# Two-layer modulated transformer on one core: the last batch's query and key rows move to another buffer, and every engine gets a new written-out order

## The chip, the cores and the metric

The kernel runs on one core of one Trainium2 chip. The metric is the device time of one execution in microseconds (us). TensorE is PE in the profile, its weight loads PEld, VectorE DVE, ScalarE ACT, GpSimd POOL, SyncE SP.

## What is computed

Input x has 8 batches of 512 rows of 128 floats, all in float32. Two layers follow one another, and in both every sublayer is of the same form: `x = x + gate * sublayer(layernorm(x) * (1 + scale) + shift)`, where shift, scale and gate are rows of `silu(c) @ wmod`, one set for each batch.

- Layer 0, attention: 16 heads of 8 elements, queries and keys rotated, softmax over 512 keys.
- Layer 0, experts: 8 experts with `silu(h @ w0) * (h @ w1) @ wo`, weighted by a softmax over the best two of 8 gate logits.
- Layer 1, gated unit: `qk = silu(normed @ W_qk + b_qk)`, `q = qk * gamma0 + beta0`, `k = qk * gamma1 + beta1`, `sim = q.T @ k / 512` (a 256x256 matrix per batch), `attn = softmax(sim)`; with `v, gate = silu(normed @ W_hidden + b_hidden)` the result is `(v * sum(attn, -1)) * gate @ W_out + b_out`.
- Layer 1, feed-forward: each batch is one expert's share: `gelu(h @ w1[b] + b1[b]) @ w2[b] + b2[b]`.

## The kernel before, in words

The program works batch by batch, in four stages: P (normalise, project, rotate, and split queries and keys into three bf16 parts), A (attention), B (experts), C (all of layer 1). A step such as C6.sim is step `sim` of stage C for batch 6; a number behind it is a group, chunk or half (C6.dn0 is the first half of the down-projection, C7.up2 the third chunk of the up-projection). Stages of several batches run beside one another: while PE is in the experts of batch b it also works on the attention of batch b+1 and on layer 1 of an earlier batch.

Nothing decides at run time what comes next. `SLOTS` (line 69) holds for each step and engine a list of positions, batch after batch (and within a batch, instance after instance, as `INSTANCES` lists them); `order_of` (line 305) sorts them, and `walk` (line 543) emits the steps of an engine in that order. Only the order of the numbers counts. Steps that exist in one batch alone (for instance `C.out0` and `C.upb`, in the last batch) have numbers for the others that emit nothing. Waits between engines are on semaphores, written by `after(engine, name, batch, count)`; an engine that waits holds up all that stands behind it in its order.

PSUM has eight banks: `sm` and `se` (two banks each, the two score products of attention), `pv` (weighted values), `wp` (experts), `m0` (shared by A and B, `shared_ab`) and `m1` (shared by P and C, `shared_pc`). In the last batch attention is over, so stage C of batch 7 uses other banks than `m1`: `qk` goes to `wp` and `pv`, the four hidden chunks to `sm` and `se`, `sim` to `m0`, `out` to `wp`, `up` to `sm` and `se`, `dn` to `m0`, `m1`, `wp`, `pv`.

Steps that the change and the prediction touch, in the tail:

- `q_and_k` (line 632): from the silu'd rows z, four instructions per half (lines 644, 645, 647, 649) write q and k to the tile `kq` of 128 x 2 x 4 x 256. It is on DVE for batch 7, on POOL for the others.
- `gl`, the gelu output of the feed-forward, is the same memory as `kq` (line 464). So `q_and_k` of batch b waits for both halves of the down-projection of batch b-1, which reads `gl` (line 635).
- `eo` (line 410), 128 x 8 x 2 x 128, holds the output weights of the experts. It is loaded once and read by step B.down (lines 1030 to 1031), last in batch 7.
- `sim` (line 1078) multiplies q by k on PE (L1088), `simmax`, `simexp` and `simsum` (lines 1748, 1341, 1755) make its softmax and the scaled output weights `wos`, `hids` (line 1726) makes v times gate (`vg`, L1730 and L1735), `c_out` (line 1102) multiplies them, `res` (line 1773) adds the residual.
- `dn` (line 1141) is the down-projection (L1159, in the last batch L1149), `fin` (line 1799) its last addition, on DVE; the output store `outp` and then the load of the next down-projection's weights `loadd` stand behind it on SP; `w2g` (line 1933) scales those weights on POOL.
- `out0` (line 1092) and `upb` (line 1117) start the sums of batch 7 in PSUM ahead of time: x2 through the identity, and the bias rows of `up`.
- `stats3`, `rstd3`, `xn3`, `xT3`, `nT3` are the second normalisation: statistics on DVE, power on POOL (L1854), scaling on DVE in batch 7 (L1584), transposes on PE (L889), modulation on ACT (L1234); then `up` (L1134 in batch 7), `upa` and `upg` (L1782, L1792).

Steps of the start: `P.xT` (L889), `P.v` (L915), `P.xn` on ACT for batches after the first (L1249), `e0hi` and `e1hi` (L1196, L1201) round the expert weights on ACT, `e1lo` (L1847) takes the rest on POOL; `A.max` (L932 on PE, L1557 on DVE) is the pass that finds each row's largest score, `A.exp` (L956 on PE, L1269 on ACT) the pass that exponentiates.

The last part of the order of PE, read off `SLOTS`, before:

```
C6.up0 B7.down71 C6.up1 C6.up2 C6.up3 C7.xT C7.qk0 C6.dn0 C7.qk1 C6.dn1 C7.hid0 C7.out0 C7.hid2
C7.upb0 C7.hid1 C7.hid3 C7.sim C7.upb1 C7.out C7.xT3 C7.up0 C7.up1 C7.up2 C7.up3 C7.dn0 C7.dn1
```

## Time and profile before

| | |
|---|---|
| median of 3 runs | 1085.66 us (1082.01 to 1087.82) |
| the profiled execution | 1092.12 us |
| its span, first to last instruction | 1089.9 us, mean granted TensorE clock 0.930 |
| busy: PE, PEld, DVE, ACT, POOL | 85%, 47%, 71%, 60%, 39% |

The profiled execution is 6.46 us (0.6%) above the median of the three; 2.2 us of its time lie outside the span. The profile's views used below are the page (busy shares, and the span in 40 slices), stretches (busy time and granted clock of each engine in a window), the chain of waits that ended last, the timeline (instructions in order, with the idle time of the engine ahead of them and what ended it) and the list of who waited for whom. A granted clock of 1.00 is 2.4 GHz and 0.50 is 1.2 GHz.

### The profile page before, as it was taken

Reading aid. Unit: us, or ns where it says so; the run is one execution under the profiler, and the core shown is the slowest. Engines: PE = TensorE matmul, PEld = TensorE weight load, DVE = VectorE, ACT = ScalarE, POOL = GpSimd, SP = SyncE. Lnnn points to the kernel's source line nnn. Section 1 sums busy time; section 2 is a strip of 40 time slices with the busy share of each in tenths; the row PEclk is TensorE's granted clock in tenths of the full one; section 3 lists DMA queues with packets and bytes.
Section 4 is the critical chain, followed back from the end, with each engine's and each line's share of the span. In section 5 each row is a group of like instructions: output and inputs, shape, how many; then the busy total and the mean of one; then the engine's idle time right before and its main releaser. Section 6 shows DMA issues by size and latency. Waiting matters only on the chain. (4 is left out here: it accounts for less than half of the span.)

```text
span 1089.9 us, 15616 instructions
## 1 busy us (share of the span) xinstructions
PE 926.0 (85%) x5176; PEld 513.5 (47%) x5176; DVE 776.2 (71%) x1467; ACT 655.6 (60%) x1176; POOL 426.8 (39%) x537
## 2 busy tenths in 40 slices
PE   4247678997899799998999998999998999889785
PEld 2111135443444355554554654446464466368553
DVE  6566678677756877788867777888878765546665
ACT  1236664666656758668768576866856756745441
POOL 2161042226112815574134364653556244454300
PEclk9558988999999989999999999999999899979876
DMA  8520304001300140111300014150001000010010
GB/s 233 154 66 30 60 30 98 33 1 55 59 2 1 32 101 9 34 43 58 62 1 13 16 61 86 59 105 11 1 25 33 2 21 16 20 35 1 18 34 10
DMA packets 54536, 47.09 MB, mean 43 GB/s; under 512 B 12393, under 2 KB 50025, under 8 KB 53114
## 3 DMA queue, kind: packets, MB, share of 16 engines
q1 hardware_dynamic: 53898, 45.85, 16.7%
q8 instruction: 42, 0.69, 0.3%
q14 instruction: 36, 0.29, 0.1%
q10 hardware_dynamic: 560, 0.26, 0.1%
HBM read 30.97 MB, written 14.73 MB: 42 GB/s over the span
## 5 line engine op out<-in xcount | busy, mean ns | idle before, releaser
L1557 DVE TENSOR_REDUCE negmax<-scores_for_max 128x2 f32<-128x1024 f32 x252 | 307.9, 1222 | 73.7 <-PE scores_for_max L932 71.3
L1269 ACT ACTIVATE probs<-scores 128x1024 f32<-128x1024 f32 x256 | 262.0, 1023 | 91.8 <-PE scores L956 90.7
L1030 PE MATMUL shared_ab<-eo,mu 128*128 128x128 f32 x1024 | 143.4, 283 | 9.0 <-ACT scaled L1383 4.8
L1030 PEld LDWEIGHTS shared_ab<-eo,mu 128*128 128x128 f32 x1024 | 129.0, 193 | 45.2 <-issue 28.1
L966 PE MATMUL weighted_values<-probs,vaug 128*32 128x512 f32 x1024 | 142.3, 630 | 1.0 <-ACT probs L1269 0.9
L1953 POOL TENSOR_TENSOR acc<-acc,scaled 128x512 f32<-128x512 f32 x55 | 71.2, 1294 | 178.8 <-ACT scaled L1383 178.7
L1692 DVE SCALAR_TENSOR_TENSOR mu<-th,expert_units 128x512 f32<-128x512 f32 x112 | 76.7, 685 | 72.4 <-ACT th L1311 71.6
L932 PE MATMUL scores_for_max<-ks,qs 48*128 48x512 bf16 x504 | 102.6, 404 | 27.8 <-DVE negmax L1557 19.4
L572 PE MATMUL expert_units<-hb_hi,e_lo 128*128 128x512 f32 x224 | 112.2, 501 | 15.3 <-DVE mu L1692 9.7
L956 PE MATMUL scores<-qs,ks 51*128 51x512 bf16 x512 | 102.2, 396 | 20.8 <-ACT probs L1269 17.7
L1311 ACT ACTIVATE th<-expert_units 128x512 f32<-128x512 f32 x112 | 66.8, 597 | 78.8 <-PE expert_units L574 77.2
L1698 DVE TENSOR_TENSOR mu<-mu,expert_units 128x512 f32<-128x512 f32 x112 | 76.5, 683 | 31.1 <-PE expert_units L574 30.5
L1383 ACT ACTIVATE scaled<-shared_ab,pick 128x128 f32<-128x128 f32 x220 | 68.5, 365 | 44.8 <-PE shared_ab L1030 41.4
L573 PE MATMUL expert_units<-hb_lo,e_hi 128*128 128x512 f32 x224 | 89.9, 402 | 0.0
L574 PE MATMUL expert_units<-hb_hi,e_hi 128*128 128x512 f32 x224 | 89.6, 400 | 0.0
L572 PEld LDWEIGHTS expert_units<-hb_hi,e_lo 128*128 128x128 f32 x224 | 42.6, 190 | 87.2 <-DVE mu L1698 28.6
L932 PEld LDWEIGHTS scores_for_max<-ks,qs 48*128 48x128 bf16 x504 | 24.6, 94 | 111.8 <-DVE negmax L1557 70.9
L956 PEld LDWEIGHTS scores<-qs,ks 51*128 51x128 bf16 x512 | 25.0, 94 | 88.2 <-ACT probs L1269 47.6
L1909 POOL CAST mpart<-negmax 128x16 bf16<-128x16 f32 x32 | 8.8, 274 | 142.0 <-DVE negmax L1557 141.9
L574 PEld LDWEIGHTS expert_units<-hb_hi,e_hi 128*128 128x128 f32 x224 | 42.9, 192 | 10.1
L573 PEld LDWEIGHTS expert_units<-hb_lo,e_hi 128*128 128x128 f32 x224 | 43.3, 193 | 0.9 <-issue 0.5
L1139 PE MATMUL shared_pc<-xdn,w 128*128 128x512 f32 x56 | 32.1, 657 | 9.4 <-ACT u L1366 8.9
(320 smaller groups left out, 1590.8 us busy)
## 6 DMA issues: line engine op xcount, KB each, us to landing
parts_d<-parts SPq DMA_DIRECT2D x15, 384.0 KB, 2.5
qs<-parts_d SPq DMA_DIRECT2D x14, 384.0 KB, 6.1
ks<-parts_d SPq DMA_DIRECT2D x14, 384.0 KB, 9.8
w<-in_L_ffn_w SPq DMA_DIRECT2D x16, 256.0 KB, 3.9
parts_d<-parts SPq DMA_DIRECT2D x15, 256.0 KB, 2.7
...
```

Of the source, the lines that this page charges most:

```text
L572: nc.tensor.matmul(out_ap, w_lo, x_hi, start=True, stop=False)
L573: nc.tensor.matmul(out_ap, w_hi, x_lo, start=False, stop=False)
L574: return nc.tensor.matmul(out_ap, w_hi, x_hi, start=False, stop=True)
L932: last = nc.tensor.matmul(max_bank(b, g, n)[:, 512 * m:512 * (m + 1)], qs[at, b % 2, p, t * P:(t + 1) * P], ks[at, b % 2, p, :], start=Tru ...
L956: last = nc.tensor.matmul(se[:, 512 * m:512 * (m + 1)], ks[at, b % 2, p, kt * P:(kt + 1) * P], qs[at, b % 2, p, :], start=True, stop=True)
L966: last = nc.tensor.matmul(pv[32 * j:32 * j + 32, :], vaug[:, kt, PAIRS * (j // 2) + GP * g + j % 2, :], probs[:, kt % 2, j % 2, j // 2, :] ...
L1030: last = nc.tensor.matmul(m0[:, at], mu[:, (2 * e + f) % 4, at], eo[:, e, f, :], start=(f == 0), stop=(f == HALVES - 1))
L1269: nc.scalar.activation(probs[:, kt % 2, j, :, :].rearrange("p m s -> p (m s)"), se[:, :], ACT.Exp)\
L1557: V.tensor_reduce(negmax[:, g % 2, :, n], max_bank(b, g, n)[:, :].rearrange("p (m s) -> p m s", m=2), AX, ALU.max, negate=True)\
L1692: V.scalar_tensor_tensor(out=mu[:, u % 4, :], in0=th[:, u % 2, :], scalar=1.0, in1=w0p(b, u), op0=ALU.add, op1=ALU.mult).then_inc(sig["b_u ...
L1698: V.tensor_tensor(mu[:, u % 4, :], mu[:, u % 4, :], w1p(b, u), ALU.mult).then_inc(sig["b_mu"], 1)
L1953: G.tensor_tensor(acc[:, :, :], acc[:, :, :], scaled[:, :, :], ALU.add).then_inc(sig["b_acc"], 1)
```

## The change

Two edits of the code, and a new set of positions.

1. In batch 7, q and k are written to the memory of `eo`, and `sim` reads them there. The first half of `q_and_k` waits for the last read of `eo` (16 counts of `b_down`) and no longer for the down-projection of batch 6. Since batch 7's `gl` still lies in `kq`'s memory, the wait for batch 6's down-projection moves to the first `upg` of batch 7.
2. The second set of modulation columns on PE waits until DVE has copied the first.
3. All of `SLOTS` is new. The set of steps on each engine is the same; of 1288 steps on PE 831 stand at another place, by at most 9 places; on DVE 412 of 834, by up to 47; on ACT 506 of 824, by up to 19; on POOL 150 of 250, by up to 10; on SP 75 of 114, by up to 9.

```diff
@@ SLOTS, some of the lines @@
-    ("P", "stats"): dict(dve=(78, 184, 192, 215, 297, 363, 549, 571)),
+    ("P", "stats"): dict(dve=(76, 142, 205, 226, 295, 361, 549, 571)),
-    ("P", "xT"): dict(pe=(27, 54, 68, 181, 325, 532, 658, 881)),
+    ("P", "xT"): dict(pe=(30, 60, 72, 178, 324, 531, 662, 880)),
-    ("P", "e0hi"): dict(act=(25, 32, 33, 34, 39, 40, 41, 59)),
+    ("P", "e0hi"): dict(act=(20, 21, 24, 27, 38, 45, 46, 50)),
-    ("C", "stats2"): dict(dve=(361, 481, 555, 701, 780, 853, 936, 1000)),
+    ("C", "stats2"): dict(dve=(363, 482, 555, 703, 781, 853, 934, 1000)),
-    ("C", "qk"): dict(pe=(471, 477, 595, 605, 821, 829, 944, 965, 1070, 1074, 1176, 1183, 1262, 1269, 1325, 1327)),
+    ("C", "qk"): dict(pe=(472, 480, 594, 603, 822, 828, 945, 961, 1069, 1073, 1177, 1183, 1262, 1274, 1325, 1326)),
-    ("C", "sim"): dict(pe=(526, 637, 874, 1002, 1111, 1215, 1301, 1335)),
+    ("C", "sim"): dict(pe=(526, 637, 873, 1002, 1111, 1215, 1299, 1332)),
-    ("C", "dn"): dict(pe=(598, 600, 813, 818, 952, 958, 1065, 1067, 1172, 1174, 1257, 1259, 1326, 1328, 1343, 1344)),
-    ("C", "fin"): dict(dve=(517, 519, 646, 649, 735, 738, 808, 811, 882, 884, 937, 939, 1006, 1012, 1031, 1032)),
+    ("C", "dn"): dict(pe=(597, 599, 812, 819, 952, 958, 1065, 1067, 1172, 1175, 1258, 1259, 1327, 1333, 1343, 1344)),
+    ("C", "fin"): dict(dve=(515, 519, 645, 650, 735, 738, 809, 811, 883, 885, 938, 939, 1012, 1016, 1031, 1032)),
-    ("C", "rstd3"): dict(pool=(107, 134, 172, 198, 223, 237, 261, 272)),
-    ("C", "w2g"): dict(pool=(23, 146, 168, 196, 217, 239, 254, 271)),
+    ("C", "rstd3"): dict(pool=(104, 138, 171, 197, 222, 238, 263, 271)),
+    ("C", "w2g"): dict(pool=(34, 136, 167, 201, 220, 234, 257, 272)),
-    ("C", "upb"): dict(pe=(8, 9, 13, 14, 15, 16, 17, 18, 31, 34, 37, 43, 49, 51, 1332, 1336)),
-    ("C", "out0"): dict(pe=(6, 7, 10, 11, 12, 33, 50, 1330)),
+    ("C", "upb"): dict(pe=(1, 3, 4, 5, 6, 7, 13, 14, 15, 16, 17, 18, 19, 20, 1336, 1337)),
+    ("C", "out0"): dict(pe=(2, 8, 9, 10, 11, 12, 41, 1334)),
...
@@ code @@
+        def kq_of(b):
+
+            return eo[:, :, :, :].rearrange("p e f d -> p (e f d)").rearrange("p (a t n) -> p a t n", a=2, t=NT) if b == LAST else kq
+
         def q_and_k(eng, E, b, p):
             after(eng, "c_qs", b, p + 1)
             if p == 0:
-                after(eng, "c_dn", b - 1, 2)
+                if b == LAST:
+                    after(eng, "b_down", b, 2 * NEX)
+                else:
+                    after(eng, "c_dn", b - 1, 2)
                 if b == 0:
                     eng.wait_ge(s_small, 3)
-            at = slice(2 * p, 2 * p + 2)
+            at, kq = slice(2 * p, 2 * p + 2), kq_of(b)
...
                     pe.wait_ge(s_silu, 2 * (L + 1))
                     if L:
                         pe.wait_ge(s_cr, 16 * N_CONST)
+                        pe.wait_ge(s_cols, 2)
...
-                        last = nc.tensor.matmul(dst[:, n * QK:(n + 1) * QK], kq[:, 0, t, n * P:(n + 1) * P],
-                                                kq[:, 1, t, :], start=(t == 0), stop=(t == NT - 1))
+                        last = nc.tensor.matmul(dst[:, n * QK:(n + 1) * QK], kq_of(b)[:, 0, t, n * P:(n + 1) * P],
+                                                kq_of(b)[:, 1, t, :], start=(t == 0), stop=(t == NT - 1))
...
             def upg(b, c):
                 after(dve, "c_ut", b, c + 1)
                 if b == LAST:
+                    if c == 0:
+                        after(dve, "c_dn", b - 1, 2)
```

The last part of the order, after, for PE and DVE (`fin` is C6.fin0 and C6.fin1; on POOL `C7.w2g` goes from ahead of `C7.rstd3` to behind it):

```
PE   C6.up3 C7.xT C7.qk0 C7.qk1 C6.dn0 C7.hid0 C7.hid2 C7.hid1 C7.hid3 C7.sim C6.dn1 C7.out0 C7.out
     C7.upb0 C7.upb1 C7.xT3 C7.up0 C7.up1 C7.up2 C7.up3 C7.dn0 C7.dn1
DVE  C6.upg3 C7.qks0 C7.qkgb0 C7.qks1 C7.qkgb1 C7.hids0 C7.hids2 C6.fin0 C7.hids1 C7.simmax C7.hids3
     C6.fin1 C7.simsum C7.keep C7.res C7.stats3 C7.xn3 C7.keep3 ...
```

On DVE before it was `C6.upg3 C6.fin0 C7.qks0 C7.qks1 C7.qkgb0 C7.qkgb1 C7.hids0 C6.fin1 C7.hids2 C7.hids1 C7.simmax C7.hids3 C7.simsum`, the rest as after. At the start, PE's `P1.v A0.max00 P1.proj1 A0.max01 ... A0.max07 P2.xT A0.max10` takes the place of `A0.max00 P1.v A0.max01 P1.proj1 A0.max02 A0.max03 A0.max04 P2.xT A0.max05 ... A0.max10`. When batch 7 enters stage B, DVE's `C5.upa3 C6.stats2 C5.upg3 B7.x1 B7.stats C5.fin0 C5.fin1` takes the place of `C5.upa3 C5.upg3 B7.x1 C6.stats2 C5.fin0 B7.stats C5.fin1`, and PE's `C7.row` goes from between C5.dn0 and C5.dn1 to ahead of B7.oT.

## Rows read from the trace of the kernel before

**Rows 1.** The page: busy time, share and instructions of each engine.
```profile
PE 926.0 (85%) x5176; PEld 513.5 (47%) x5176; DVE 776.2 (71%) x1467; ACT 655.6 (60%) x1176; POOL 426.8 (39%) x537
```

**Rows 2.** A stretch of 50 us: length, busy us (x instructions) by engine, clock, DMA.
```profile
50.00:100.00 50.00, 26.10 (x124) 8.76 (x123) 34.39 (x45) 21.78 (x34) 22.65 (x27) 0.62 0.20 64
```

**Rows 3.** The chain that ended last, in order of time: start, us, what.
```profile
1042.08 2.08 PE expert_units L1051 x4
1044.15 3.07 PE shared_pc L1159 x16
...
1048.09 1.80 PE shared_pc L1159 x16
...
1049.98 0.69 DVE kq L644
```

**Rows 4.** Timeline of the tail: hidden chunks, sim, vg alone and beside POOL's w2g, upb.
```profile
1054.89 1.98 PE L1068 MATMUL scores<-xcn,rot 128*128 128x512 f32 x4
...
1056.46 0.69 DVE L1735 TENSOR_TENSOR vg<-probs 128x512 f32<-128x512 f32 x1
...
1056.71 3.62 PE L1088 MATMUL shared_ab<-kq 128*128 128x256 f32 x16
...
1060.26 1.98 PE L1124 MATMUL scores<-ones,rem 1*128 1x512 f32 x4
...
1061.42 1.55 POOL L1935 TENSOR_TENSOR w<-w,cgb 128x512 f32<-128x512 f32 x1 [23.17 <-DMA w<-in_L_ffn_w]
...
1061.89 1.64 DVE L1735 TENSOR_TENSOR vg<-probs 128x512 f32<-128x512 f32 x1
...
1063.45 0.15 DVE L1757 RECIPROCAL cst<-cst 128x2 f32<-128x2 f32 x1
```

**Rows 5.** Timeline of the tail from out on.
```profile
1065.28 3.75 PE L1112 MATMUL expert_units<-wos,vg 128*128 128x128 f32 x16 [3.04 <-issue]
...
1072.47 1.11 DVE L1584 TENSOR_SCALAR xdn<-x,mv_d,rstd_d 128x128 f32<-128x128 f32 x4 [1.12 <-POOL rstd_d L1854]
...
1073.64 1.12 PE L889 MATMUL weighted_values<-ident,xdn 128*128 128x128 f32 x4 [4.62 <-DVE xdn L1584]
...
1075.63 3.78 PE L1134 MATMUL scores_for_max<-xdn,w 128*128 128x512 f32 x4 [0.87 <-ACT xdn L1234]
...
1083.52 1.47 DVE L1792 SCALAR_TENSOR_TENSOR kq<-probs,scores 128x512 f32<-128x512 f32 x2
```

**Rows 6.** Stretches of 1 us, columns as in Rows 2; the granted clock follows POOL.
```profile
1046.00:1047.00 1.00, 1.00 (x8) 1.00 (x7) 0.00 (x0) 0.00 (x0) 0.00 (x0) 0.64 0.00 0
...
1063.00:1064.00 1.00, 0.00 (x0) 0.00 (x0) 0.96 (x3) 0.00 (x0) 0.84 (x1) 0.89 0.00 0
```

**Rows 7.** The chain: when batch 7's down-projection weights were loaded.
```profile
1057.34 4.01 DMA w<-in_L_ffn_w
```

**Rows 8.** Timeline of the start: e1lo on POOL, and what waited behind it.
```profile
60.29 4.60 POOL L1847 TENSOR_TENSOR e_lo<-probs,e_hi 128x2048 fp32r<-128x2048 f32 x1 [1.13 <-ACT e_hi L1201]
...
68.64 1.11 PE L889 MATMUL shared_pc<-ident,xp 128*128 128x128 f32 x4 [4.41 <-ACT xp L1249]
...
70.34 1.23 DVE L1557 TENSOR_REDUCE negmax<-scores 128x2 f32<-128x1024 f32 x1 [4.51 <-PE scores L932]
```

**Rows 9.** Timeline where batch 7 enters stage B: C5.upg3, C6.mod, C5.dn0.
```profile
955.96 0.91 DVE L1796 SCALAR_TENSOR_TENSOR kq<-u,uz 128x512 f32<-128x512 f32 x1 [2.77 <-ACT u L1392]
...
956.40 1.59 POOL L630 TENSOR_TENSOR hc<-hc,crow 128x512 f32<-128x512 f32 x1
...
957.39 3.62 PE L1159 MATMUL shared_pc<-w,kq 128*128 128x128 f32 x16
```

**Rows 10.** Who waited for whom on PE, 100 to 880 us: us, times, longest.
```profile
PE scores L956 <- ACT probs L1269: 15.3, 28, 1.2
...
PE expert_units L572 <- DVE mu L1692: 9.5, 15, 3.5
```

**Rows 11.** A stretch of 20 us after batch 0's attention, columns as in Rows 2.
```profile
160.00:180.00 20.00, 17.46 (x73) 8.71 (x73) 17.01 (x42) 5.72 (x11) 3.23 (x6) 0.76 0.34 88
```

More of the change, by code:

```diff
@@ L255 @@
-    ("C", "out"): dict(pe=(539, 647, 886, 1012, 1117, 1227, 1308, 1337)),
-    ("C", "res"): dict(dve=(476, 547, 692, 773, 845, 916, 980, 1019)),
-    ("C", "stats3"): dict(dve=(484, 559, 694, 774, 849, 918, 982, 1020)),
-    ("C", "rstd3"): dict(pool=(107, 134, 172, 198, 223, 237, 261, 272)),
-    ("C", "xn3"): dict(act=(336, 413, 552, 635, 706, 776, 839, 846), dve=(28, 32, 33, 34, 35, 36, 73, 1021)),
-    ("C", "xT3"): dict(pe=(564, 771, 902, 1026, 1135, 1237, 1317, 1338)),
-    ("C", "nT3"): dict(act=(340, 471, 560, 639, 707, 779, 845, 864)),
@@ L294 @@
[L294 to L300 removed]
+    ("P", "load"): dict(sp=(1, 19, 28, 31, 48, 57, 79, 84)),
@@ new lines @@
+    ("A", "wog"): dict(dve=(255, 339, 420, 534, 602, 731, 792, 924)),
+    ("B", "load"): dict(sp=(21, 55, 65, 77, 89, 103, 118, 128)),
+    ("B", "oT"): dict(pe=(169, 323, 477, 633, 786, 944, 1108, 1256)),
+    ("B", "ot"): dict(act=(109, 198, 283, 390, 480, 590, 693, 797)),
+    ("B", "y"): dict(pe=(170, 326, 479, 636, 793, 951, 1112, 1257)),
+    ("B", "x1"): dict(dve=(268, 356, 438, 540, 631, 733, 841, 936)),
+    ("B", "stats"): dict(dve=(269, 357, 440, 541, 633, 734, 842, 937)),
+    ("B", "rstd"): dict(pool=(37, 68, 89, 127, 152, 190, 217, 247)),
@@ new lines @@
+    ("B", "x2"): dict(pool=(64, 86, 123, 151, 187, 215, 241, 242), dve=(48, 49, 50, 51, 52, 53, 55, 992)),
+    ("C", "load"): dict(sp=(44, 70, 80, 100, 111, 119, 127, 132)),
+    ("C", "loadu"): dict(sp=(25, 82, 91, 107, 115, 125, 130, 133)),
+    ("C", "loadd"): dict(sp=(29, 75, 95, 112, 116, 124, 131, 135)),
+    ("C", "stats"): dict(dve=(354, 436, 545, 640, 740, 838, 929, 994)),
+    ("C", "rstd"): dict(pool=(66, 94, 129, 159, 194, 218, 243, 268)),
+    ("C", "xn"): dict(act=(201, 325, 402, 549, 633, 699, 795, 838), dve=(1, 2, 3, 4, 5, 6, 7, 996)),
@@ new lines @@
+    ("C", "out"): dict(pe=(538, 647, 885, 1012, 1117, 1227, 1307, 1335)),
+    ("C", "res"): dict(dve=(476, 547, 691, 773, 845, 916, 981, 1019)),
+    ("C", "stats3"): dict(dve=(480, 558, 692, 774, 848, 918, 982, 1020)),
+    ("C", "rstd3"): dict(pool=(104, 138, 171, 197, 222, 238, 263, 271)),
+    ("C", "xn3"): dict(act=(336, 429, 552, 634, 704, 776, 840, 847), dve=(47, 63, 67, 68, 89, 98, 99, 1021)),
+    ("C", "xT3"): dict(pe=(564, 768, 899, 1024, 1133, 1239, 1317, 1338)),
+    ("C", "nT3"): dict(act=(341, 472, 561, 637, 708, 780, 846, 864)),
@@ new lines @@
+    ("P", "e1hi"): dict(act=(49, 58, 59, 60, 85, 95, 100, 146)),
+    ("P", "whhi"): dict(act=(25, 28, 29, 33, 34, 43, 44, 102)),
+    ("P", "small"): dict(act=(30, 31, 32, 36, 40, 41, 48, 54)),
+    ("P", "e1lo"): dict(pool=(13, 15, 17, 18, 19, 20, 25, 39)),
+    ("P", "mod1"): dict(dve=(123, 194, 218, 222, 240, 244, 264, 298)),
+    ("P", "whlo"): dict(dve=(157, 166, 171, 174, 190, 200, 213, 266)),
+    ("P", "e0lo"): dict(dve=(176, 177, 180, 186, 193, 196, 197, 223)),
+    ("P", "modst"): dict(sp=(6, 7, 8, 9, 10, 12, 14, 15)),
```

224 lines of the change are left out of this document (100 added, 124 removed), and 176 rows, old and new, of the table SLOTS.

## The prediction

> **What bounds the kernel now.** I read the busy table first: PE is at work 85% of the span [rows 1], so outside start and tail it sets the pace, and a saving must be fewer waits of PE or less of the half-rate clock. The stretches then show where it isn't busy: 26.1 us of the 50 from 50 to 100 us, at a mean clock of 0.62 [rows 2]. The other such place is the tail, so I read there the chain that ended last and the timeline. The chain runs qk0 on PE, the first half of batch 6's down-projection, the second half at 1048.09 to 1049.89, and then DVE's first instruction on kq at 1049.98 [rows 3]: kq's memory was held by gl until dn1 was done. After it come sim, which ends at 1060.33, simsum from 1063.45, out from 1065.28 to 1069.03, and the second normalisation [rows 4, 5]. All this is sequential work, and PE does out at half rate, 3.75 us for 16 products, as dn1 needs 1.80 for 16 of the same shape [rows 3, 5].
>
> **The tail, step by step.** Up to qk0's end at 1044.15 I take times as they are.
>
> *Sim.* Once the wait is gone, DVE may write kq as soon as qk0 has passed ACT and qks. Two qks and eight instructions on kq at up to 0.69 us each [rows 3] make 6.9 us; from about 1045 they end by 1052. PE's queue now is qk1, dn0, four hidden chunks, sim. qk1 at half rate takes qk0's 2.1, to 1046.2. Full rate was granted during the microsecond from 1046, after PE had been busy since 1042.08 [rows 3, 6]; dn0 lies across that, I take 2.1 (between 1.80 and 3.07), to 1048.3. Two hidden chunks took 1.98, so four take 4.0, to 1052.3. Sim takes 3.62 [rows 4] and ends at 1055.9, not 1060.33: **-4.4**. So PE's order, not kq, is what sim then waits for; out0, the first upb and dn1 have been moved behind it, and each has to be paid or covered below.
>
> *From sim to out.* Before, 3.1 us pass from sim's end to simsum. In them vg took 1.64 where the one before it took 0.69, beside w2g on POOL (1.55) [rows 4]; w2g is moved away from here. But fin1 now stands ahead of simsum, and waits for dn1, which comes behind sim: 1.9 for dn1 and some 0.4 to 0.6 for fin1, so 2.5: **-0.6**. Out0 (8 small products, about 1.0) runs in that shadow.
>
> *Out's clock.* Before, PE stood idle from 1062.24, the clock fell within the microsecond from 1063 [rows 4, 6], and out took 3.75. Now out0 ends about 1.4 us before out can start, a little under the 1.6 or so after which it fell. I take full rate, 1.9 as dn1: **-1.85**; the other end is nothing.
>
> *Upb.* All four bias rows now stand between out and xT3: 1.98 for two, 4.0 for four at full rate. From out's end to xT3 lie 4.6 us (1069.03 to 1073.64) [rows 4, 5]: **0**, hidden by the statistics on DVE and POOL. At half rate they would be 8 and delay xT3 by 3.4. They also keep PE busy, so that xT3 (1.12) should take 0.6, **-0.5**, and the first two ups 2.0 and not 3.78 [rows 5]. From the first up's start (1075.63) to the last upg's end (1084.99) were 9.4 us; at full rate the alternation of ACT and DVE, about 0.65 a step, sets it, roughly 7.2: **-2.2**.
>
> *W2g.* On POOL it comes behind rstd3, so it starts as DVE's xn3 does (1.11 for four pieces, right after POOL's power) [rows 5]. Its weights are no worry: their load ended 4.0 us after issue [rows 7], and fin1 comes 3 us earlier than before. No row shows xn3 beside POOL. The bounds are nothing and 2.4 (w2g's 1.55 and the small one behind it); I take **+1.0**, the 0.95 that vg lost [rows 4], and keep both ends. The Trainium skill, page "SBUF — State Buffer", section "Who interferes with whom", says that DVE and POOL have one shared pair of ports, locked for a whole instruction, by a DVE instruction with two SBUF inputs or in a 2-port mode. The vg row agrees. By that page's list tensor_scalar, which is what xn3 is, can be in such a mode: the term would be up to 2.4, the sum 1.4 worse.
>
> The tail: -4.4 - 0.6 - 1.85 - 0.5 - 2.2 + 1.0 = **-8.55**.
>
> **Where batch 7 enters B.** C6.stats2 now stands on DVE ahead of C5.upg3 and B7.x1. It needs C6.mod, whose last instruction ended at 957.99, while upg3 ran at 955.96 and dn0 at 957.39 [rows 9]. Stats2 is 1.3 and upg3 0.7, so dn0 starts near 960, 2.4 late. C7.row has gone from between the two dn halves, and B7.stats no longer stands behind fin0; that gives some back. Taken **+1.5**, between -0.5 and +3. In return downd1 and x2 stand ahead of one C6.upa0 (0.6 to 0.7, as L1735 alone [rows 4]) on the way to C7: **-0.6**.
>
> **The start.** P2.xT stood in PE's queue ahead of A0.max05. It waited 4.41 us for ACT's xn, which waited for POOL, busy with e1lo for 4.60, and DVE stood 4.51 us at the next max [rows 8]. Now P2.xT comes behind max07, so the scores go on: up to -4.5. The edit of e0hi (earlier on ACT) and P1.stats (earlier on DVE) helps batch 1 along by 1 to 2 us, while P1.v ahead of max00 and P1.proj1 ahead of max01 cost about as much. Since exp must wait for the same DMA and PE has other work to catch up on, I let about half persist: **-2.5**, between 0 and -5.7. The new wait on s_cols is for two tiny copies that were done before PE came there: 0.
>
> **The middle.** All orders differ, but by few places. From 100 to 880 us PE waited 15.3 us for exp in 28 waits and 9.5 us for the gated units in 15 [rows 10]. I counted in both orders where two such steps stand closer than the other engine needs (1.5 us between exps, 1.7 between maxes, 0.85 from a w1 to the next w0). For batches 1 to 7 there are 32 places before and 37 after for exp, 52 and 52 for max; from w1 to w0 20 and 27, from w0 to w1 17 and 9. I take **+1.0**, between -2 and +5: alike.
>
> **Sum.** -8.55 + 1.5 - 0.6 - 2.5 + 1.0 = -9.15. The durations are of the profiled execution (1092.12, span 1089.9), in whose terms this is 1083.0. The three runs' median is 1085.66, to which I apply it: **1076.5 us**. A measurement of this kernel can tell about 0.5%, 5.4 us, from no change.
>
> **Rivals.**
> - *The clock falls before out.* The idle time there, 1.4 us, is close to where it fell before. Then out stays at 3.75 (+1.85) and part of upb runs at half rate and delays xT3 by 0 to 3.4 (taken 1.6): the sum is -5.7, **1080 us**. For it speaks the small margin; against it that PE is busy without a break for 15 us ahead. Chance 0.20.
> - *The wait is only exchanged.* Sim comes early because dn1, out0 and upb were put behind it; if they all come back on the path (fin1 ahead of simsum by 1.9 more, four upbs at half rate, 3.4, xn3 blocked, 2.4), the tail gains under 1 and the total is near **1084 us**. Chance 0.12.
> - *The start's gain persists whole.* With -5.7 there and nothing lost at 955 us: **1071 us**. Chance 0.13.
> - *Slower: the clock drops at the stage changes.* Place: y and the transposes of each batch, where PE waits on ACT and DVE. At 160 to 180 us such a drop gave a clock of 0.76 over 20 us [rows 11], that is 9.6 us at half rate, 4.8 of full-rate work lost if PE is busy throughout; I price it at half of that, 2.4. If the new order makes each of the seven stage changes idle long enough for one more drop, 7 x 2.4 = 16.8, -9.15 + 16.8 = +7.7, **1093 us**; it decides above 5.4 from the seventh and cancels the gain from the fourth. Against it: the counts of close places are alike. Chance 0.08.
> - *The forecast*: 0.47.
>
> **How the numbers follow.** Low end 1068: start whole (-3.2 more), no block of xn3 (-1), nothing lost at 955 us (-1.5), middle -2 (-3), not all at once. High end 1088: the clock rival with the w2g block in full, +3 at 955 us and the middle at +5 (1.4, 1.5 and 4 more). Faster by over 0.5% is under 1080.2: the forecast case mostly (0.40 of 0.47), half of the clock rival, the persisting start: 0.63. Slower than 1091.1: 0.08, with a little for what I haven't seen, 0.09. The rest, 0.28, is within.
>
> **What would show it.** In the changed kernel's tail: DVE's kq instructions start near 1045.5 of the old time scale, before dn0 ends; sim follows the last hidden chunk without a gap; out's 16 products in 1.9 us; upb at full rate with its end before xn3's; the first two ups in 2 us; xn3 over 1.11 us if POOL blocks it; DVE idle at fin1, waiting for dn1. At the start: no idle of 4 us ahead of a max, and max07 some 4 us earlier. Near 960 us: dn0 some 2 us later against y. What would make me wrong: a middle from 150 to 940 us that differs by more than 5 us in length, or out at 3.75 us.

## The result, and the profile after

The changed kernel takes 1074.49 us (median of 4 runs, 1069.84 to 1075.01) against 1085.84 us for the kernel before beside it: a ratio of 0.989, 95% interval 0.9852 to 0.9929, 11.35 us less. Forecast were 1076.5 us, and 1068 to 1088. The sign and the size came out; the terms, as will be seen, did so only in part. The profiled execution of after took 1075.01 us (span 1072.8), 0.5 above its median, where the one of before lay 6.5 above its own; so a difference of the two traces, 17.1 us, shows 6 us too much, all of it ahead of the tail. Of tail_only's twelve runs below, two took 1303.23 and 1672.69 us; its ratio leaves them out, and so does its median here, 1077.80 (1079.68 with them, from which the 4.4 us in the expectation of after_again comes).

Line numbers have moved by 7 to 10: L1088 is now L1096, L1112 L1120, L1584 L1592, L1134 L1142, L1735 L1743, L1935 L1945. First the busy table and the stretch from 50 to 100 us of after (columns as in [rows 1] and [rows 2]):

```profile
PE 916.9 (85%) x5176; PEld 507.8 (47%) x5176; DVE 773.2 (72%) x1467; ACT 656.1 (61%) x1176; POOL 428.5 (40%) x537
```

```profile
50.00:100.00 50.00, 29.74 (x126) 8.75 (x124) 31.88 (x42) 21.24 (x30) 19.22 (x25) 0.59 0.11 35
```

PE is 9 us less busy than in [rows 1] with the same 5176 instructions: less of its work fell to the half rate. The start has the low clock that it had, 0.59 after 0.62. Then the tail, the timeline of after from batch 7's queries on:

```profile
1031.88 2.08 PE L1059 MATMUL expert_units<-wqk,xcn 128*128 128x256 f32 x4 [1.51 <-ACT xcn L1242]
...
1035.35 0.69 DVE L651 TENSOR_TENSOR eo<-th,gam 128x512 f32<-128x512 f32 x1
...
1035.46 2.21 PE L1167 MATMUL shared_pc<-w,kq 128*128 128x128 f32 x16
...
1040.29 0.69 DVE L656 TENSOR_TENSOR eo<-eo,bet 128x512 f32<-128x512 f32 x1
...
1041.04 3.32 PEld L1096 LDWEIGHTS shared_ab<-eo 128*128 128x128 f32 x16 [0.77 <-DVE eo L654]
1041.08 3.69 PE L1096 MATMUL shared_ab<-eo 128*128 128x256 f32 x16
...
1049.10 2.02 PE L1120 MATMUL expert_units<-wos,vg 128*128 128x128 f32 x16 [1.65 <-DVE wos L1777]
...
1053.13 1.95 PE L1132 MATMUL scores<-ones,rem 1*128 1x512 f32 x4
...
1054.50 1.26 POOL L1945 TENSOR_TENSOR w<-w,cgb 128x512 f32<-128x512 f32 x1
1054.57 2.20 DVE L1592 TENSOR_SCALAR xdn<-x,mv_d,rstd_d 128x128 f32<-128x128 f32 x4 [1.12 <-POOL rstd_d L1864]
...
1056.83 1.11 PE L897 MATMUL weighted_values<-ident,xdn 128*128 128x128 f32 x4 [1.74 <-DVE xdn L1592]
...
1058.81 3.78 PE L1142 MATMUL scores_for_max<-xdn,w 128*128 128x512 f32 x4 [0.87 <-ACT xdn L1242]
```

The queries and keys (`eo` now) are made from 1035.35, before dn0 has even begun, and no longer after dn1 [rows 3]. Measured from the start of qk0, sim ends at 12.89 us where it ended at 18.25 [rows 3, 4], 5.36 earlier. The last key row is ready at 1040.98, only 0.1 us before sim starts, and sim's first weight load stood idle 0.77 us for these rows: DVE's chain and PE's queue now end together. Out starts 4.33 after sim's end (4.95 before, to [rows 5]), and takes 2.02 for 3.75. Then it turns: xn3 takes 2.20 beside w2g, not 1.11, and xT3 starts 5.71 after out's end, not 4.61. xT3 and the first ups are at half rate as before (1.11 and 3.78). The stretches of 1 us around it, columns as in [rows 6]:

```profile
1055.00:1056.00 1.00, 0.08 (x1) 0.00 (x0) 1.00 (x2) 0.00 (x0) 1.00 (x2) 1.00 0.00 0
1056.00:1057.00 1.00, 0.17 (x1) 0.18 (x2) 0.90 (x4) 0.00 (x0) 0.18 (x1) 0.74 0.00 0
1057.00:1058.00 1.00, 0.94 (x4) 0.54 (x4) 0.57 (x1) 0.02 (x1) 0.00 (x0) 0.50 0.00 0
```

The clock was still 1.00 in the microsecond from 1055, and fell in the next. In the start, the timeline of DVE after:

```profile
74.14 1.23 DVE L1565 TENSOR_REDUCE negmax<-scores_for_max 128x2 f32<-128x1024 f32 x1 [1.32 <-PE scores_for_max L940]
...
81.57 1.23 DVE L1565 TENSOR_REDUCE negmax<-scores_for_max 128x2 f32<-128x1024 f32 x1 [4.27 <-PE scores_for_max L940]
```

The idle time of 4.5 us at 70 us [rows 8] is gone, and another of 4.27 stands at 77 to 82 us, while PE takes up the exp pass. So the start's lead is real and soon eaten into.

### The profile page after: what moved, and what is told of

The parts are those of the page before. It is cut to its first block and busy times, and to the rows that moved or that the text cites. A ratio compares the mean times of both kernels' runs of the same rounds, so it can differ in the third digit from the quotient of the medians.

```text
span 1072.8 us, 15618 instructions
## 1 busy us (share of the span) xinstructions
PE 916.9 (85%) x5176; PEld 507.8 (47%) x5176; DVE 773.2 (72%) x1467; ACT 656.1 (61%) x1176; POOL 428.5 (40%) x537
## 5 line engine op out<-in xcount | busy, mean ns | idle before, releaser
L1565 DVE TENSOR_REDUCE negmax<-scores_for_max 128x2 f32<-128x1024 f32 x252 | 307.6, 1221 | 67.9 <-PE scores_for_max L940 66.0
L1038 PE MATMUL shared_ab<-eo,mu 128*128 128x128 f32 x1024 | 141.1, 281 | 3.7 <-ACT scaled L1391 2.0
L1700 DVE SCALAR_TENSOR_TENSOR mu<-th,expert_units 128x512 f32<-128x512 f32 x112 | 76.7, 685 | 66.1 <-ACT th L1319 65.6
L964 PE MATMUL scores<-qs,ks 51*128 51x512 bf16 x512 | 102.2, 396 | 25.4 <-ACT probs L1277 23.7
L1319 ACT ACTIVATE th<-expert_units 128x512 f32<-128x512 f32 x112 | 66.9, 597 | 83.0 <-PE expert_units L574 81.8
L964 PEld LDWEIGHTS scores<-qs,ks 51*128 51x128 bf16 x512 | 25.1, 94 | 106.4 <-ACT probs L1277 59.5
L974 PEld LDWEIGHTS weighted_values<-probs,vaug 128*32 128x32 f32 x1024 | 20.8, 110 | 44.0 <-issue 34.9
```

The costliest lines, as they stand in the source:

```text
L964: last = nc.tensor.matmul(se[:, 512 * m:512 * (m + 1)], ks[at, b % 2, p, kt * P:(kt + 1) * P], qs[at, b % 2, p, :], start=True, stop=True)
L974: last = nc.tensor.matmul(pv[32 * j:32 * j + 32, :], vaug[:, kt, PAIRS * (j // 2) + GP * g + j % 2, :], probs[:, kt % 2, j % 2, j // 2, :] ...
L1038: last = nc.tensor.matmul(m0[:, at], mu[:, (2 * e + f) % 4, at], eo[:, e, f, :], start=(f == 0), stop=(f == HALVES - 1))
L1565: V.tensor_reduce(negmax[:, g % 2, :, n], max_bank(b, g, n)[:, :].rearrange("p (m s) -> p m s", m=2), AX, ALU.max, negate=True)\
L1700: V.scalar_tensor_tensor(out=mu[:, u % 4, :], in0=th[:, u % 2, :], scalar=1.0, in1=w0p(b, u), op0=ALU.add, op1=ALU.mult).then_inc(sig["b_u ...
```

## The experiments

Four theories. **T1**: the gain is made in the tail, by the place of steps; the buffer only permits it. **T2**: it is made ahead of the tail. **T3**: xn3 and PE's clock took back what the tail's terms promised. **T4**: batch 7's entry into B costs time, the start wins some. The table has what the traces of all kernels show: the ends of the 8th, 24th and 256th `max` (L1557 or L1565), the clock from 90 to 106 us, the starts of batch 7's first expert product (scores<-hb_hi) and of qk0, and the span's end, in us.

| kernel | 8th max | clock | 24th max | 256th max | first expert product | qk0 | end |
|---|---|---|---|---|---|---|---|
| before | 73.8 | 0.89 | 105.6 | 905.9 | 971.3 | 1042.1 | 1089.9 |
| before_again | 73.2 | 0.50 | 109.9 | 904.3 | 971.3 | 1042.7 | 1091.3 |
| code_only | 73.1 | 0.71 | 107.6 | 897.6 | 963.0 | 1033.7 | 1081.3 |
| tail_only | 74.6 | 0.89 | 105.9 | 896.5 | 962.4 | 1033.2 | 1074.4 |
| rest_only | 65.9 | 1.00 | 102.2 | 893.2 | 959.6 | 1028.5 | 1075.2 |
| after | 66.9 | 0.79 | 106.1 | 897.3 | 965.6 | 1031.9 | 1072.8 |
| after_again | 67.2 | 0.79 | 106.4 | 898.2 | 966.3 | 1032.5 | 1073.3 |
| w2g_late | 66.3 | 1.00 | 102.6 | 893.5 | 962.1 | 1030.0 | 1070.6 |
| hot_tail | 66.6 | 0.58 | 106.6 | 897.9 | 964.3 | 1033.1 | 1075.3 |
| hot_both | 66.1 | 1.00 | 102.4 | 892.6 | 960.8 | 1031.1 | 1071.8 |
| entry_old | 66.9 | 0.79 | 106.1 | 895.4 | 964.5 | 1032.0 | 1072.8 |
| head_old | 74.4 | 0.89 | 105.8 | 897.3 | 963.7 | 1030.0 | 1070.9 |
| hot_fit | 66.4 | 1.00 | 102.6 | 890.9 | 957.3 | 1026.1 | 1063.7 |
| hot_upb0_first | 66.3 | 1.00 | 102.6 | 893.9 | 962.5 | 1030.5 | 1071.0 |

### Taking the change apart: code_only, tail_only, rest_only

The first has the code of after and all the positions of before. The other two splice the two sets of positions where the same steps have been emitted on each engine in both: PE after C7.qk0, and the corresponding places on the others. On PE, `tail_only` against the kernel before:

```diff
 C6.up0 B7.down71 C6.up1 C6.up2 C6.up3 C7.xT C7.qk0
-C6.dn0 C7.qk1 C6.dn1 C7.hid0 C7.out0 C7.hid2 C7.upb0 C7.hid1 C7.hid3 C7.sim C7.upb1 C7.out C7.xT3
+C7.qk1 C6.dn0 C7.hid0 C7.hid2 C7.hid1 C7.hid3 C7.sim C6.dn1 C7.out0 C7.out C7.upb0 C7.upb1 C7.xT3
```

On DVE ten places of the tail change with it, and on POOL C7.w2g and C7.rstd3 change places; ACT's order in the tail is the same. In `rest_only` it is the other way about: the minus line follows the order of after.

> The order of before throughout; only the buffer of the last batch's queries and keys, and what the kernel loads for it, are those of after. If the place of steps makes the gain, nothing is won: the masked keys can be made half a microsecond earlier, but the similarity product stands behind other matmuls in PE's own queue, so 1085 to 1086. If the buffer itself makes it (the keys are free earlier), 1080 to 1082.

> The order of before up to the last batch's tail; from there, with the buffer, the order of after. The tail theory (the gain is made behind batch 7's queries and keys) expects the tail as in after: 41.75 us from the start of its last query transposes' batch work to the end where before shows 48.65, and a time 6.9 us under before's, about 1079. The rival, that the gain was made by the other moved steps ahead of the tail, expects 1084 to 1086 here, with the tail's gain given back in the batches' phases.

> The order of after up to the tail, with the buffer; in the tail the order of before. The tail theory expects what is left of the 11 us, 3 to 5: about 1081.5. My prediction's start (2.5 of lead) less its middle and entry (1.0 and 1.5) expects 1085.5. The rival that puts the gain ahead of the tail expects 1075 to 1077.

Measured, beside one another on one chip (before 1084.08): code_only 1083.95, ratio 1.0015 (0.9989 to 1.0042); tail_only 1077.80, ratio 0.9968 (0.9934 to 1.0001); rest_only 1076.87, ratio 0.9944 (0.9915 to 0.9974). The buffer alone brings nothing. (The new order of the tail can't be run without it: dn1 stands behind sim there, sim needs the keys, and by the old wait the keys need dn1.) The timeline of code_only shows why:

```profile
1045.23 0.68 DVE L656 TENSOR_TENSOR eo<-eo,bet 128x512 f32<-128x512 f32 x1
...
1046.55 1.98 PE L1076 MATMUL scores<-xcn,rot 128*128 128x512 f32 x4
...
1048.37 3.62 PE L1096 MATMUL shared_ab<-eo 128*128 128x256 f32 x16
```

The last key row is ready at 1045.91, and sim starts 2.5 us later, behind the hidden chunks; from qk0's start to sim's are 14.65 us, as in before (14.63). The same interval in tail_only and in rest_only:

```profile
1033.18 2.08 PE L1059 MATMUL expert_units<-wqk,xcn 128*128 128x256 f32 x4 [1.51 <-ACT xcn L1242]
...
1042.51 3.62 PE L1096 MATMUL shared_ab<-eo 128*128 128x256 f32 x16
```

```profile
1028.48 2.07 PE L1059 MATMUL expert_units<-wqk,xcn 128*128 128x256 f32 x4 [1.51 <-ACT xcn L1242]
...
1043.55 3.62 PE L1096 MATMUL shared_ab<-eo 128*128 128x256 f32 x16
```

These are 9.33 us with the new tail and 15.07 with the old. From qk0 to the end the table gives 46.7 to 48.6 us for the four kernels with the old tail (mean 47.7) and 40.8 to 41.2 for tail_only, after, after_again, entry_old and head_old (40.9): **-6.8** for the tail. By its ratio tail_only is 0.3% faster (0 to 0.7%), which includes 6.8 us at its end only; by its median it is 6.3 us. The rest, however, won 6.1 us by its ratio: rest_only's 1076.87 lies under the 1081.5 that I had expected, within the 1075 to 1077 of the rival, and my own terms for it come to 0.6. Both T1 and T2 are half right.

### How far one trace can be trusted: before_again, after_again

Both kernels unedited, traced once more; after_again was also timed.

> The kernel before, traced a second time. Its profiled execution was 6.3 us above its median. If that is chance, spread over the middle phases, this trace reaches batch 7's tail 4 to 6 us earlier than the first, at 1036 to 1038 us for the first product of head pair 0, and the tail itself is again 48.6 long. If the middle of before is always that long, it stands at 1042 again.

> The changed kernel again, beside the three below on one chip. If the gain of 11 us is the change's own, 1073 to 1075; if some of it was luck of those few runs, as the two pieces (4.4 and 7.2 less in medians, 6.4 to 7.3 less in the tail by the traces) leave possible, up to 1077. The tail again 40.9 long from the first query product, the stretch from batch 7's x1 to there 79.6 again (80.3 with the old tail, 83.7 to 84.7 in the orders of before).

before_again took 1093.34 us, with 48.5 us from qk0 to the end (47.9 in before), and reached qk0 at 1042.7: not 4 to 6 us earlier. Yet 29 runs of this kernel beside it had a median of 1084.08, and code_only, which has its order, reached qk0 at 1033.7. Two of the 29 were as long, 1093.15 and 1093.30. So both traces of before are of its longest executions, which I take for chance. Between the 24th and the 256th max they took 800.4 and 794.4 us; code_only and tail_only, in the same order, 790.0 and 790.5; and all ten kernels in the order of after 788.2 to 791.7. The middle of the two orders is alike in these twelve; what made it 4 to 10 us longer in the two traces of before isn't known. after_again took 1071.47 us (1070.41 to 1075.46), ratio 0.9877 (0.9849 to 0.9904): the gain is the change's own.

### What took back part of the tail's gain: w2g_late

```diff
             def w2g(b):
                 after(pool, "c_ind", b, 48)
+                if b == LAST:
+                    after(pool, "c_xn3", b, 1)
```

> POOL's last w2g waits until DVE's xn3 is done. If xn3's 2.20 us was the shared port, it takes 1.11 again, and xT3 starts 1.1 us earlier relative to out. If xn3 is slow for another reason (its own place right behind POOL's power), it stays at 2.2. The idle time of PE ahead of xT3 shrinks from 1.74 to about 0.65: if the clock fell for that idle time alone, xT3 (0.6) and the ups (2.0 a pair) come at full rate and the kernel is 3 us faster; if not, 1.1 us faster. By the medians 1.1 can't be told, by the trace of the tail it can: 39.8 or about 38 from the first query product to the end.

1072.81 us, ratio 0.9887 (0.9858 to 0.9915), like after. Its timeline:

```profile
1051.27 3.54 PE L1132 MATMUL scores<-ones,rem 1*128 1x512 f32 x4
...
1052.70 1.12 DVE L1592 TENSOR_SCALAR xdn<-x,mv_d,rstd_d 128x128 f32<-128x128 f32 x4 [1.12 <-POOL rstd_d L1864]
...
1053.96 1.26 POOL L1947 TENSOR_TENSOR w<-w,cgb 128x512 f32<-128x512 f32 x1 [1.29 <-DVE xdn L1592]
...
1054.74 1.11 PE L897 MATMUL weighted_values<-ident,xdn 128*128 128x128 f32 x4
```

xn3 is back at 1.12 with nothing else changed about it: 1.08 us were w2g's. So the block is shown. (The Trainium skill, page "SBUF — State Buffer", section "Who interferes with whom", has POOL and DVE exclude one another when DVE's instruction is in a 2-port mode, and counts tensor_scalar among those that can be; the measured 2.20 and 1.12 agree.) But little came of it in this trace: the clock fell during the second pair of bias rows (3.54 for 1.95), xn3 ended at 1053.82, and xT3 stood behind them until 1054.74. From out's end it starts 5.49 later, 0.22 better than after's 5.71. Taking away one wait exposed the next, and the tail was 40.6. That goes with the clock: it fell in the second pair also in tail_only and head_old, which have the block (there xT3 starts 5.79 and 5.77 after out's end). In hot_fit below, which has this edit too, it held through both pairs, and xT3 starts 4.62 after out's end: all of the 1.09 us is back.

### What holds the clock: hot_tail, hot_both, hot_fit, hot_upb0_first

All four have w2g_late's edit, and products of the identity by itself, whose results nothing reads:

```diff
+            def hot(bank, n):
+                for _ in range(n):
+                    nc.tensor.matmul(bank[:, 0:P], ident[:, :], ident[:, :], start=True, stop=True)
...
                     last.then_inc(sig["c_begun"], 1)
+                    if h == 1:
+                        after(pe, "c_out", b - 1, 2)
+                        hot(m1, 5)

             def up(b, c):
+                if b == LAST and c == 0:
+                    hot(m1, 9)
```

> As the run before, and PE multiplies the identity by itself into a free bank, 5 times behind upb and 9 times behind xT3, so that it hardly stands idle. If my term for the ups was right in its reason and only the idle time took it away, the first two ups take 2.0 instead of 3.78, and up's start to the last gated unit 7.2 instead of 9.0: tail 37.5 to 38. If ACT and DVE set that stretch anyway, it stays at 9.0 with the clock at full, and the tail at 39.3 or above.

1073.49 us, ratio 0.9886 (0.9859 to 0.9913). The timeline of hot_tail:

```profile
1057.66 2.50 PE L888 MATMUL shared_pc<-ident 128*128 128x128 f32 x10
...
1063.66 1.88 PE L1151 MATMUL scores_for_max<-xdn,w 128*128 128x512 f32 x4
```

The ups are at full rate, 1.88 a pair, and from their start to the end of the span are 11.6 us where after has 14.0: **-2.3**. From the first up's start to the last gated unit's end it is 7.0, where I had forecast 7.2. But the price was misjudged: each of these products is two instructions and takes 0.5 us at half rate (2.50 for five) and 0.23 at full (6.86 for thirty in hot_both), so 14 of them delayed xT3 and the ups by more than they won, and the tail was 42.2.

In hot_both there were 74 more, behind C6.up1, up2, up3 and C7.xT:

```diff
                 nc.tensor.matmul(m1[:, :], w1[:, at], nt3, start=True, stop=True).then_inc(sig["c_up"], 1)
+                if b == LAST - 1 and c > 0:
+                    after(pe, "b_mu", LAST, UNITS)
+                    hot(hid_bank[0], (30, 24, 10)[c - 1])
...
             def qk(b, p):
+                if b == LAST and p == 0:
+                    hot(hid_bank[0], 10)
```

> As the run before, with 74 more such products: 30, 24 and 10 behind batch 6's up products 1, 2 and 3, and 10 behind batch 7's transposes. The two query products (2.08 and 1.91) and the down-projection half behind them (2.21) then run at full rate, 1.0, 1.0 and 1.8. DVE's eight instructions on the queries and keys end 7.0 us after the first of them ends and become what the similarity product waits for: 1.6 to 1.8 us less in all, best case 1068 to 1070. The other way: the extra products delay the real ones or bring the chip's throttle down elsewhere, and it is no faster than the run before.

1075.56 us, ratio 0.9916 (0.9892 to 0.9941): the extra products delayed the real ones. From the first expert product to qk0 are 70.3 us, not 66.3 to 68.9, and the expected 1068 to 1070 did not come. Yet the clock was 1.00 throughout from 1010 to 1040 us, and qk0 took 1.03 us, which in after is at half rate (2.08). With half as many:

```diff
-                    hot(hid_bank[0], (30, 24, 10)[c - 1])
+                    hot(hid_bank[0], (17, 14, 6)[c - 1])
-                    hot(hid_bank[0], 10)
+                    hot(hid_bank[0], 5)
-                        hot(m1, 5)
+                        hot(m1, 1)
-                    hot(m1, 9)
+                    hot(m1, 5)
             def c_out(b):
+                if b == LAST:
+                    after(pe, "c_out", b - 1, 2)
+                    hot(m1, 6)
```

> The products that keep the clock up, with counts that fit (one costs 0.23 us at full rate, twice what I had assumed): 17, 14, 6 and 5 where there were 30, 24, 10 and 10, 6 ahead of out, 1 ahead of xT3 and 5 behind it. The steps of batch 6's up product are then where they were, the query products and the half down-projection take 1.0, 1.0 and 1.95, the similarity product ends 1.7 earlier, xT3 takes 0.6, the ups 1.9 a pair: tail 35 to 36 from the first query product where the changed kernel has 40.9 (one of those us is the queries' own start), and 1066 to 1069 in all. If the clock falls during the one-row products again, as in the two runs with the late w2g, 1.5 more.

The profiled execution took 1065.74 us, the shortest of all runs here, and its tail 37.6 us, not 35 to 36; the median of six, 1072.94, is outside the expected 1066 to 1069, and its ratio, 0.9898 (0.9868 to 0.9927), is no better than that of after. Its timeline:

```profile
1026.05 1.13 PE L1065 MATMUL expert_units<-wqk,xcn 128*128 128x256 f32 x4 [0.85 <-ACT xcn L1259]
...
1034.30 3.69 PE L1102 MATMUL shared_ab<-eo 128*128 128x256 f32 x16 [1.03 <-DVE eo L654]
...
1042.32 2.02 PE L1129 MATMUL expert_units<-wos,vg 128*128 128x128 f32 x16
...
1048.96 1.11 PE L901 MATMUL weighted_values<-ident,xdn 128*128 128x128 f32 x4 [0.19 <-DVE xdn L1609]
```

qk0 takes 1.13 for 2.08, and sim now waits 1.03 us for DVE's key rows. But sim starts only 0.95 us earlier from qk0's start than in after (8.25 for 9.20), because in after the keys were ready only 0.1 us before sim: DVE's chain sets the time at once, as expected. And xT3 is at half rate again, with hardly a gap ahead of it: something else than idle time let the clock fall. The last kernel tries the bias rows themselves:

```diff
-C7.out0 C7.out C7.upb0 C7.upb1
+C7.out0 C7.upb0 C7.out C7.upb1
             def c_out(b):
-                if b == LAST:
-                    after(pe, "c_out", b - 1, 2)
-                    hot(m1, 6)
-                        hot(m1, 1)
+                        hot(m1, 8)
```

> As the run before, but the first pair of one-row products stands ahead of out, in place of the 6 identity products, and 8 identity products follow the second pair. Out starts 0.35 late. If the one-row products let the clock fall when four of them follow each other, it stays at full here and the kernel is 1 us faster than the run before; if the fall has another cause, it is 0.3 slower.

1073.43 us, ratio 0.9888 (0.9856 to 0.992), and the opposite of the hope: it doesn't take four one-row products in a row. Its timeline, and its stretches of 1 us:

```profile
1045.18 1.95 PE L1138 MATMUL scores_for_max<-ones,rem 1*128 1x512 f32 x4
...
1047.06 2.50 PE L1126 MATMUL expert_units<-wos,vg 128*128 128x128 f32 x16
...
1049.49 3.78 PE L1138 MATMUL scores<-ones,rem 1*128 1x512 f32 x4
```

```profile
1046.00:1047.00 1.00, 1.00 (x3) 0.18 (x1) 0.99 (x3) 0.00 (x0) 0.00 (x0) 1.00 0.93 271
1047.00:1048.00 1.00, 1.00 (x9) 0.95 (x9) 0.92 (x2) 0.00 (x0) 0.00 (x0) 1.00 0.18 29
1048.00:1049.00 1.00, 1.00 (x9) 1.00 (x9) 0.00 (x0) 0.00 (x0) 0.00 (x0) 0.75 0.69 183
```

PE is busy without a gap from 1046, by the record, and the clock falls in the middle of out, behind one pair of one-row products. In every kernel with the new tail it has fallen by xT3 at the latest, in w2g_late, hot_tail, hot_both, tail_only and head_old already in the second pair (2.88 to 3.67 instead of 1.95). What all these falls have ahead of them are one-row products (1x512, one of 128 rows of the array in use), which began some 2 to 5.5 us earlier. But in the four traces with the old tail one pair of them, in two halves from 1052.42 to 1054.96 in before, had no fall behind it: the clock stayed at 1.00 through sim. So the one-row products are the suspect and no more; no run had them replaced by full ones of the same length, and by this run's own expectation another cause is left open.

### The entry and the start: entry_old, head_old

`entry_old` changes the order of ten steps on DVE alone:

```diff
-C6.stats C5.upa2 C5.upg2 A7.onorm3 C5.upa3 C6.stats2 C5.upg3 B7.x1 B7.stats C5.fin0
+C5.upa2 C6.stats C5.upg2 A7.onorm3 C5.upa3 C5.upg3 B7.x1 C6.stats2 C5.fin0 B7.stats
```

> The changed kernel with ten steps of DVE, at batch 7's entry into B, in the order of before: batch 7's statistics again behind batch 5's fin0, which waits for the down-projection, and batch 6's stats2 behind x1. My forecast's +1.5 for the entry says that the old order is better there: x1 to the first query product would take 78 to 79 us, below 79.6. The other theory, that the statistics behind fin0 were what batch 7's scores waited for, expects it 1.5 to 2 longer than 79.6 to 80.3, with most of the 3.1 us between x1's end and the statistics back. In the median under 2 us either way.

1075.46 us, ratio 0.992 (0.9893 to 0.9948). Timelines, first of after and then of entry_old (L991 on PE is y, the last product of batch 7's attention, which x1 reads):

```profile
948.55 2.05 PE L991 MATMUL shared_ab<-ga,pvs 128*128 128x128 f32 x8 [1.52 <-ACT pvs L1228]
...
949.88 0.87 DVE L1540 BATCH_NORM_STATS2 stats_c<-hc 128x6 f32<-128x128 f32 x4 [1.16 <-POOL hc L630]
...
951.66 0.68 DVE L1638 TENSOR_TENSOR x<-shared_ab,x 128x512 f32<-128x512 f32 x1
...
952.38 0.87 DVE L1540 BATCH_NORM_STATS2 stats_b<-x 128x6 f32<-128x128 f32 x4
```

```profile
948.12 0.77 DVE L1794 SCALAR_TENSOR_TENSOR u<-u,uz 128x512 f32<-128x512 f32 x1 [4.16 <-ACT u L1374]
...
948.71 2.05 PE L991 MATMUL shared_ab<-ga,pvs 128*128 128x128 f32 x8 [3.64 <-ACT pvs L1228]
...
950.80 0.69 DVE L1638 TENSOR_TENSOR x<-shared_ab,x 128x512 f32<-128x512 f32 x1 [0.23 <-PE shared_ab L991]
...
954.67 0.86 DVE L1540 BATCH_NORM_STATS2 stats_b<-x 128x6 f32<-128x128 f32 x4
```

In after, stats2 does wait for POOL (1.16) and x1 is late behind it, as the forecast had it: x1 starts 1.06 us after y's end, and in the nine traces with this order 1.06 to 1.98; dn0 starts 1.2 to 2.1 after y's end where in the old order it starts within 0.2 of it. In entry_old x1 follows y at once again (0.04), as in the four kernels in the old order. So the mechanism of the forecast is shown, and so is what the new order buys with it: batch 7's statistics follow x1 at once in after, and stand 3.2 us off in entry_old, behind fin0.

Nothing was won back, because y itself came later. It starts 49.6 to 50.9 us after the 256th max in the old order, 51.2 in all nine traces of the new, and 53.3 in entry_old, where PE waits 3.64 us for ACT's pvs and DVE 4.16 (2.43 in after) for ACT's u, the last up-product of batch 5. What made those late was not tried. From x1's end to qk0 are 80.5 us in entry_old and 79.5 in after; but w2g_late and head_old, with the same order in that stretch as after, have 81.5 and 77.6, so one trace can't tell 1 us there, and neither my 78 to 79 nor the other theory's 1.5 to 2 more is settled.

From the 256th max to the first expert product the table gives 65.3 to 67.0 us for the four kernels in the old order (mean 65.9) and 66.4 to 68.6 for the nine in the new (67.5): the entry costs **+1.6** in the mean. The nine fall into two groups, four at 66.4 to 66.5 and five at 68.1 to 68.6, with the same order.

`head_old` has the order of before on every engine up to about 115 us (PE up to A1.exp020, DVE up to B0.x1), and then that of after. On PE, from the 11th step on:

```diff
-P1.v A0.max00 P1.proj1 A0.max01 A0.max02 A0.max03 A0.max04 A0.max05 A0.max06 A0.max07 P2.xT
+A0.max00 P1.v A0.max01 P1.proj1 A0.max02 A0.max03 A0.max04 P2.xT A0.max05 A0.max06 A0.max07 P2.v
```

> The changed kernel with the order of before up to about 115 us on every engine. If the start's gain persists by half, as forecast, it is 2.5 slower than the changed kernel, 1074.5 to 1076; if the lead of 7 us at the eighth max is all lost again by the clock and by what PE has to catch up on, 1072 to 1073.5; if it persists whole, 1078 or more. By the trace the eighth max stands at 73 to 74 us instead of 66 to 67.

1075.66 us, ratio 0.9919 (0.9891 to 0.9948); the start is worth 1.2 to 4.2 us by the medians of after and after_again, and 2.5, the forecast, is near the middle of that. (The runs are not all of one chip; by the ratios it is 3.1 and 4.6 us, and the intervals overlap.) The table shows where the other half goes. At the 8th max the new order leads by about 7 us in every trace (65.9 to 67.2 against 73.1 to 74.6). At the 24th it stands at 102.2 to 102.6 in five traces and at 106.1 to 106.6 in four, and the old order at 105.6 to 109.9. The stretch from 90 to 106 us tells them apart; first rest_only, then head_old:

```profile
90.00:106.00 16.00, 11.60 (x81) 2.80 (x81) 10.26 (x10) 10.57 (x13) 1.99 (x5) 1.00 0.15 52
```

```profile
90.00:106.00 16.00, 12.09 (x79) 2.60 (x77) 11.45 (x11) 10.09 (x11) 1.01 (x5) 0.89 0.15 50
```

With a clock of 1.00 there, some 3.5 to 4.5 us of the lead are kept; where it is 0.79 or 0.58, less than 1 (against the mean of the old order, 107.0). The order up to there is the same each time, so that is chance. The mean over the traces is 107.0 in the old order and 104.2 in the new: **-2.8**.

### Batch 7's experts

This part got no run of its own: the table has it. From the first expert product to qk0 are 70.8 to 71.4 us in the four kernels with the old order and 66.3 to 68.9 in the nine with the new (hot_both aside): mean 70.9 and 67.6, **-3.3**. Two of the nine, hot_fit and hot_upb0_first, have extra products in this phase; without them it is -3.5. Stretches of that phase up to the last down-product in code_only and in after, and who waited for whom on PE in them (us, times, longest):

```profile
962.90:1016.80 53.90, 50.24 (x272) 41.14 (x273) 36.07 (x85) 25.92 (x64) 26.00 (x24) 0.96 0.03 10
```

```profile
965.60:1015.00 49.40, 47.73 (x271) 39.89 (x271) 35.15 (x85) 26.54 (x65) 23.27 (x21) 1.00 0.05 13
```

```profile
PE scores L572 <- DVE mu L1700: 1.3, 1, 1.3
PE shared_ab L1038 <- ACT scaled L1391: 0.8, 1, 0.8
PE shared_ab L1038 <- DVE mu L1706: 0.7, 1, 0.7
PE scores_for_max L572 <- DVE mu L1706: 0.5, 1, 0.5
```

```profile
PE shared_ab L1038 <- ACT scaled L1391: 1.4, 3, 0.7
PE scores L572 <- POOL hb_lo L1884: 0.2, 1, 0.2
```

PE is idle 3.66 us of it in the old order and 1.67 in the new: the 2.5 us in which it waited for DVE's gated units are gone. That is 2.0 us of the 4.5 between these two; the rest is a busy time 2.5 less with one instruction less in the records, which is the clock, 1.00 for 0.96.

## Why the prediction was right, step by step

By the means of the traces the parts are: start -2.8, middle 0, entry +1.6, batch 7's experts -3.3, tail -6.8. Their sum is -11.3, and the medians say -11.35. Forecast was -9.15. So the total was right in part by luck: the tail gave 1.75 us less than forecast, batch 7's experts 2.7 and the middle 1.0 more, and these errors offset each other.

- **Sim** (-4.4): right in its reason, -5.36 in size. That with the old order sim stands in PE's queue long after the keys are ready is shown by code_only (2.5 us). With the new order the queue was faster than I had it and the margin is gone: the keys are ready 9.09 us after qk0's start and sim starts at 9.19 in after, and only in tail_only (9.33) and hot_tail (9.73) is PE's queue clearly later. The size was off by 0.95, as I set PE's products end to end: qk1 took 1.91 and not 2.1, and in the record each of the four products that follow qk0 (the hidden chunks in pairs) starts 0.16 to 0.21 us ahead of the end of the one before it (0.73 in all).
- **From sim to out** (-0.6): -0.62. **Out's clock** (-1.85): -1.73; the rival in which the clock falls before out did not come. But the reason failed: PE was idle 1.65 us ahead of out, not 1.4, so longer than the 1.6 after which I had it fall, and the clock held at 1.00 in all eight traces with that gap.
- **W2g** (+1.0): the block is real, +1.09 on xn3, and shown by w2g_late. Both ends of my range missed the point that the upb products can stand right behind it: without the block 0.22 came back in w2g_late, and all of it in hot_fit. My remark that fin1 comes 3 us earlier than before goes against my own steps: it starts 15.05 us after qk0's start, for 13.33. W2g did not wait for its load all the same.
- **Upb** (0) and **the ups** (-0.5 and -2.2): this is the step of the tail that failed. "They also keep PE busy, so that xT3 (1.12) should take 0.6, and the first two ups 2.0 and not 3.78": they were busy and full rate did not last. xT3 took 1.11, the first ups 3.78, and from up's start to the last gated unit's end only 0.36 was won. That full rate there is worth 2.3 is shown by hot_tail; why the clock fell stays open. In all, the tail gave 1.75 less than forecast.
- **Entry** (+1.5): +1.6 in the mean. The reason given, stats2 ahead of x1 on DVE, is real: dn0 came 1.4 to 2.3 us later against y, and entry_old takes that away. But y also came later in the new order, by 0.3 to 1.6 us, which I had not forecast, and the early statistics gave back 3 us; so the sum has other parts than mine, and undoing one of them recovered nothing.
- **Batch 7's experts**: forecast as one small term (-0.6) and a share of the middle's +1.0; it was -3.3. Counting places that stand too close gave +1.0 for a stretch where nothing changed, and missed the three waits for the gated units that did. A count over seven batches hides what one batch gains; the last batch should have been laid out step by step like the tail. That the new order of these steps is the cause is read off the traces, not isolated.
- **Start** (-2.5): -2.8 by the traces, 1.2 to 4.2 by the medians; "about half persists" is in truth a draw between a half and nearly none. One of its signs, no idle time of 4 us ahead of a max, did not come: 4.27 us stand ahead of the one at 81.57.
- **Middle** (+1.0): 0, alike, within -2 and +5.
- **The sums of the range**: the high end's own terms come to 1086.9, not 1088, and the rival of the start to 1071.8, not 1071. Neither changes a conclusion.

Of the rivals, "the clock falls before out" and "the wait is only exchanged" would have shown in the tail and did not; "slower by clock drops at the stage changes" is out, since the middle was 788 to 792 us long in every trace of the new order.
